# Feed-forward weights turned and their low-rank products added in one PSUM bank, bias rows centred before the loops, early scales in two pieces

## The reference, cut to what matters

```python
x = x + xattn(ctx, ctx, layernorm(x))       # 128 batches x 64 tokens x 128; 16 heads; softmax over the key axis
x = x + ffn(layernorm(x))                   # gamma, beta given for the layer norms inside
# ffn, h = its input:
for blk in range(3):
    i0, i1 = 2 * blk, 2 * blk + 1
    y = qlora(h, i0); y = layernorm(y, gamma[blk], beta[blk]); y = gelu(y)
    y = qlora(y, i1); h = y + h
# qlora(x, i) = x @ W_i.T + bias_i + (x @ la_i.T) @ lb_i.T     W_i = (q_i / 7.5 - 1) * scale_i (groups of 16), rank 32
```

## Time and profile before

| what | value |
|---|---|
| median of three runs | 362.67 us |
| the profiled execution, its own time | 362.27 us |
| its span | 360.4 us |
| PE, DVE busy | 340.1 us (94%), 331.7 us (92%) |
| ACT, POOL busy | 288.2 us (80%), 266.8 us (74%) |
| chain that ended last | PE 62%, DVE 23%, POOL 5%, issue 5%, ACT 3% |

### The profile page before, as it was taken

One profiled execution on the slowest core, in us unless ns is written; L12 is line 12 of the kernel. 1 busy time (PEld: TensorE's weight loads), 2 busy tenths in 40 slices (PEclk: granted clock), 3 DMA queues, 4 the chain that ended last, 5 costly groups with the idle time before them and its releaser, 6 DMA issues.

```text
span 360.4 us, 13093 instructions
## 1 busy us (share of the span) xinstructions
PE 340.1 (94%) x4804; PEld 254.6 (71%) x4804; DVE 331.7 (92%) x821; ACT 288.2 (80%) x585; POOL 266.8 (74%) x288
## 2 busy tenths in 40 slices
PE   7888799999999999999999798988999999999995
PEld 6555367677667667766766566865888888888874
DVE  6899999999999999999999999979999999988774
ACT  4698588788788878878887767668889999999983
POOL 6609488878877977987897999878877788774231
PEclk9999899999999999999999999999999999999999
DMA  7879286467548547745834400000010000210112
GB/s 197 237 238 274 70 255 188 143 202 218 169 137 262 177 136 210 212 154 159 262 132 136 148 4 2 2 1 3 17 45 29 29 29 29 61 32 29 36 54 88
DMA packets 54531, 43.29 MB, mean 120 GB/s; under 512 B 4625, under 2 KB 48609, under 8 KB 54497
## 3 DMA queue, kind: packets, MB, share of 16 engines
q1 hardware_dynamic: 53920, 42.31, 38.8%
q10 hardware_dynamic: 576, 0.53, 0.5%
HBM read 26.05 MB, written 16.78 MB: 119 GB/s over the span
## 4 chain that ended last, share of the span: by engine, by line
PE 62%; DVE 23%; POOL 5%; issue 5%; ACT 3%; DVEq 0%; POOLq 0%; ACTq 0%
PE score_ps L1637 9%; PE att_ps L1600 7%; DVE zsum L847 6%; PE score_ps L1541 5%; DVE negmax L829 5%; PE wo_ps L1379 5%; PE score_ps L1391 3%; PE score_ps L1730 3%; PE work L1723 3%; PE work L1415 3%; POOL probs L524 3%; PE att_ps L1730 3%; PE score_ps L1631 2%; PE work L1428 2%; PE work L1421 2%
## 5 line engine op out<-in xcount | busy, mean ns | idle before, releaser
L524 POOL TENSOR_TENSOR probs<-probs,rz 128x1024 f32<-128x1024 f32 x64 | 136.2, 2141 | 37.0 <-DVE rz L850 36.9
L571 POOL TENSOR_TENSOR rs<-ve,minus_half 128x4 f32<-128x4 f32 (+1 forms) x47 | 55.6, 1184 | 34.3 <-DVE ve L778 24.7
L1139 ACT ACTIVATE probs<-score_ps 128x1024 f32<-128x1024 f32 x64 | 65.6, 1024 | 17.8 <-PE score_ps L1541 17.1
L847 DVE TENSOR_REDUCE zsum<-probs 128x64 f32<-128x1024 f32 x64 | 77.3, 1208 | 1.7 <-ACT probs L1139 1.5
L829 DVE TENSOR_REDUCE negmax<-score_ps 128x64 bf16<-128x1024 f32 x64 | 75.2, 1177 | 0.0
L1379 PEld LDWEIGHTS wo_ps<-wo_t,att_t 128*128 128x128 f32 x256 | 36.9, 191 | 13.4 <-issue 12.0
L1600 PE MATMUL att_ps<-probs,v_diag 128*32 128x64 f32 x2048 | 43.8, 225 | 2.1 <-POOL probs L524 2.1
L1637 PEld LDWEIGHTS score_ps<-lin_t,h 128*128 128x128 f32 x304 | 36.9, 191 | 11.1 <-DVE h L930 7.0
L1221 ACT ACTIVATE z<-score_ps,rs 128x128 f32<-128x128 f32 x152 | 43.5, 382 | 0.6 <-POOL rs L571 0.6
L1541 PE MATMUL score_ps<-negmax,ident_bf 128*128 128x512 bf16 x128 | 39.0, 386 | 4.7 <-DVE negmax L829 4.7
L1600 PEld LDWEIGHTS att_ps<-probs,v_diag 128*32 128x32 f32 x2048 | 33.2, 109 | 12.6 <-POOL probs L524 3.4
(11 more groups left out here) (263 smaller groups left out, 692.6 us busy)
## 6 DMA issues: line engine op xcount, KB each, us to landing
q_parts<-parts SPq DMA_DIRECT2D x15, 512.0 KB, 3.5
k_stack<-k_parts SPq DMA_DIRECT2D x30, 256.0 KB, 3.3
q_stack<-q_parts SPq DMA_DIRECT2D x60, 128.0 KB, 3.0
x_all<-in_x SPq DMA_DIRECT2D x16, 256.0 KB, 3.9
ctx_sb<-in_ctx SPq DMA_DIRECT2D x16, 256.0 KB, 3.7
k_parts<-parts SPq DMA_DIRECT2D x16, 256.0 KB, 2.9
out<-x_all SPq DMA_DIRECT2D x15, 256.0 KB, 2.3
q_parts<-parts SPq DMA_DIRECT2D x4, 128.0 KB, 2.4
```

The costliest lines, as they stand in the source:

```text
L524: nc.gpsimd.tensor_tensor(e[:, :, :, :], e[:, :, :, :], by_query.broadcast_to([P, BANDS, SEQ, ADJ]), ALU.mult).then_inc(s_probs, 1)
L571: nc.gpsimd.tensor_tensor(rs2[v][:, lo:hi], ve2[v][:, lo:hi], minus_half[:, lo:hi], ALU.pow).then_inc(p_rs[v], 1)
L847: nc.vector.tensor_reduce(zsum[q][:, :], probs[(p - 1) % 4][:, :, :, :].rearrange("p u k s -> p k u s"), AX_XY, ALU.add).then_inc(s_zsum, 1)
L1139: nc.scalar.activation(probs[p][:, :, :, :], score_ps[p % 2][:, :].rearrange("p (u s k) -> p u k s", s=ADJ, k=SEQ), ACT.Exp, scale=SCALE). ...
```

## The change

Seven things change.

1. The low-rank products are no longer added by DVE. PE turns the dequantised weight (`w_deq`) into its PSUM bank and adds the low-rank product, with operands swapped, onto it (`turned_layer`). For the even layers `lb` is turned by the product with `centre` instead of a transpose. Layers 1 to 3 are done in the prologue, layer 0 in chunk 0, pair 1, layers 4 and 5 in pair 2. L735 and L740 are gone.
2. The fold of the first layer works on `w_deq` and `la_in`, in the prologue (`folded_first_bias`).
3. The bias rows of the first layers lose their mean in the prologue (`centred_rows`, four DVE instructions ahead of the moments of chunk 1), so the seeds need only one ACT copy, in chunk 1. DVE's five instructions there are gone; its two for `res_cols` move ahead of the first key parts.
4. POOL clears `v_diag[1]` only after the first `negmax`.
5. SP loads `x_all[3]` behind the stores of chunk 1 and the fourth context behind its gathers.
6. In chunk 0 the moments and the scale of input chunk 3 move from pair 1 to pair 2.
7. The early scales are two pieces: `input_variances` (seven POOL instructions) and `input_scales` (two), at places of their own; the moments of chunks 0 and 1 move ahead.

```diff
-X_STATS = {0: (13, 0), 1: (13, 2), 2: (14, 0)}
-X_SCALES = {0: (13, 1), 1: (13, 3), 2: (14, 2)}
+X_STATS = {0: (12, 2), 1: (13, 1), 2: (14, 0)}
+X_VARIANCES = {0: (12, 3), 1: (13, 2), 2: (14, 1)}
+X_SCALES = {0: (13, 0), 1: (13, 3), 2: (14, 2)}
...
+        def moments_slot(c):
+            return 2 if isinstance(c, int) and c == 0 else 1
...
                 gather_first_q(1, s_stack[0])
-                sp.dma_start(x_all[:, 3, :, :], x_t[3]).then_inc(s_xin[3], 16)
                 store_k(1, 1)
                 store_q(1, 1)
-                sp.wait_ge(s_ctx_ps, 2)
-                sp.dma_start(ctx_sb[1][:, :, :], ctx_t[3]).then_inc(s_ctxin[1], 16)
+                sp.dma_start(x_all[:, 3, :, :], x_t[3]).then_inc(s_xin[3], 16)
                 gather_k(1, 1)
                 sp.wait_ge(s_const, 7)
                 gather_q(1, 1)
+                sp.wait_ge(s_ctx_ps, 2)
+                sp.dma_start(ctx_sb[1][:, :, :], ctx_t[3]).then_inc(s_ctxin[1], 16)
...
                 first_scale(2)
+                pool.wait_ge(s_negmax, 1)
                 clear(v_diag[1], s_vzero)
...
-                    if p == 1 and live(c + 3):
+                    if p == moments_slot(c) and live(c + 3):
                         input_variance(c + 3)
+                    input_part(X_VARIANCES, c, p, input_variances)
                     input_part(X_SCALES, c, p, input_scales)
...
+            def centred_rows():
+                nc.vector.tensor_tensor(row_mean[:, 0:1], ident[0:NROWS, ROW_BL + 2:ROW_BL + 3],
+                                        ident[0:NROWS, ROW_BL + 4:ROW_BL + 5], ALU.add)
+                nc.vector.tensor_reduce(row_mean[:, 1:2], rows[:, :], AX_X, ALU.add).then_inc(s_rows_c, 1)
+                dve.wait_ge(s_rows_c, 1)
+                nc.vector.scalar_tensor_tensor(row_mean[:, 2:3], row_mean[:, 1:2], -1.0 / D, row_mean[:, 0:1], ALU.mult,
+                                               ALU.mult).then_inc(s_rows_c, 1)
+                dve.wait_ge(s_rows_c, 2)
+                nc.vector.tensor_scalar(rows_c[:, :], rows[:, :], row_mean[:, 2:3], None, ALU.add).then_inc(s_rows_c, 1)
...
                 dve.wait_ge(s_wready, 4)
+                residual_columns()
                 dve.wait_ge(s_k_ps, 1)
...
                 next_input(0)
                 centred_query_weights()
                 bias_columns()
+                centred_rows()
                 next_input(1)
                 first_key_parts()
                 next_input(2)
                 output_weights()
+                dequantised_weights()
                 low_rank_rows()
                 bias_parts()
-                dequantised_weights()
-                last_effective_weights()
+                folded_first_bias()
...
-                    if isinstance(c, int) and (c, p) == (0, 1):
-                        effective_weights()
...
                     if isinstance(c, int) and (c, p) == (1, 0):
-                        first_layer_seeds()
+                        dve.wait_ge(s_res, 1)
...
+            def turned_layer(i, opens=False):
+                if i % 2 == 0:
+                    nc.tensor.matmul(turned_bank(i), w_deq[:, i, :], centre[:, :], start=opens, stop=False,
+                                     skip_group_check=True)
+                else:
+                    nc.tensor.matmul(turned_bank(i), w_deq[:, i, :], ident[:, :], is_transpose=True, start=opens,
+                                     stop=False, skip_group_check=True)
+                return nc.tensor.matmul(turned_bank(i), la_in[:, i, :], lb_t[:, i, :], start=False, stop=True,
+                                        skip_group_check=True)
+            def first_turned_layers():
+                pe.wait_ge(s_deq, 2)
+                pe.wait_ge(s_lbt, 1)
+                turned_layer(1, opens=True)
+                turned_layer(2)
...
                 project_k(1, 1)
-                low_rank_products(0)
+                first_turned_layers()
                 project_q(1)
                 k_remainder(1, 1)
-                low_rank_products(1)
+                turned_layer(3)
                 q_remainder(1, 1)
```

More of the change, by code:

```diff
@@ L559, in input_scales @@
                 token_variance(0, t + 1, p_xbn, p_xmv, p_xst)
+            def input_scales(t):
                 pool.wait_ge(p_xst, t + 1)
@@ L748, in effective_weights @@
                 dve.wait_ge(s_fold, 2)
+                nc.vector.tensor_scalar(la_mean[:, 1:2], la_mean[:, 0:1], -1.0 / D, None, ALU.mult).then_inc(s_fold, 1)
+                dve.wait_ge(s_fold, 3)
                 nc.vector.tensor_scalar(fold[:, 2:3], fold[:, 1:2], 1.0 / D, None, ALU.mult).then_inc(s_fold, 1)
[L750 to L767 removed]
+                dve.wait_ge(s_fold, 4)
+                nc.vector.tensor_scalar(la_in[:, 0, :], la_in[:, 0, :], la_mean[:, 1:2], None,
+                                        ALU.add).then_inc(s_fold, 1)
+                dve.wait_ge(s_fold, 5)
+                nc.vector.tensor_scalar(w_deq[:, 0, :], w_deq[:, 0, :], fold[:, 2:3], None,
+                                        ALU.add).then_inc(s_fold, 1)
             def combine_layer(v, k):
@@ L991, in transposed, with first_layer_seeds @@
                                      source[:, 0:P].rearrange("p (j h) -> p h j", j=DH), ACT.Copy).then_inc(s_wready, 1)
+            def first_layer_seeds():
+                act.wait_ge(s_seed_ps, 1)
+                nc.scalar.activation(seed[:, :, :].rearrange("p v d -> p (v d)"), wo_ps[:, 2 * P:4 * P],
+                                     ACT.Copy).then_inc(s_seed, 1)
             def transposed_layers(u):
@@ L1111, in prologue @@
                 act.wait_ge(s_wready, 4)
+                nc.scalar.activation(neg_last[:, :], cols[:, ROW_BL + 5:ROW_BL + 6].broadcast_to([P, P]), ACT.Copy,
+                                     scale=-1.0).then_inc(s_neg_last, 1)
                 first_q_part(0, 0, wo_ps, h_q_ps, h_q_hi)
@@ L1128, in prologue @@
                 q_low(1, 1)
-                nc.scalar.activation(neg_last[:, :], cols[:, ROW_BL + 5:ROW_BL + 6].broadcast_to([P, P]), ACT.Copy,
-                                     scale=-1.0).then_inc(s_neg_last, 1)
                 normalised_input(2)
@@ L1150, in chunk @@
                     input_columns(c + 2)
+                if isinstance(c, int) and c == 1:
+                    first_layer_seeds()
                 for u in range(2):
@@ L1336, in low_rank_columns @@
                 ins.then_inc(s_lbt_ps, 2)
-            def low_rank_products(u):
-                if u == 0:
-                    pe.wait_ge(s_lbt, 1)
-                else:
-                    pe.wait_ge(s_wready, 5)
-                for i in range(4 * u, min(4 * u + 4, NLIN)):
-                    ins = nc.tensor.matmul(layer_bank(i), lb_t[:, i, :], la_in[:, i, :], start=True, stop=True)
-                ins.then_inc(s_lora, 1)
-            def transpose_layers(u):
-                if u == 0:
-                    pe.wait_ge(s_weff, 3)
-                    pe.wait_ge(s_const, 5)
-                else:
-                    pe.wait_ge(s_v, 1)
-                for i in range(4 * u, min(4 * u + 4, NLIN), 2):
-                    nc.tensor.matmul(turned_bank(i), w_eff[:, i, :], centre[:, :], start=True, stop=True)
-                    ins = nc.tensor.transpose(turned_bank(i + 1), w_eff[:, i + 1, :], ident[:, :])
-                ins.then_inc(s_lint_ps, 1)
+            def turned_layer(i, opens=False):
+                if i % 2 == 0:
+                    nc.tensor.matmul(turned_bank(i), w_deq[:, i, :], centre[:, :], start=opens, stop=False,
+                                     skip_group_check=True)
+                else:
+                    nc.tensor.matmul(turned_bank(i), w_deq[:, i, :], ident[:, :], is_transpose=True, start=opens,
+                                     stop=False, skip_group_check=True)
+                return nc.tensor.matmul(turned_bank(i), la_in[:, i, :], lb_t[:, i, :], start=False, stop=True,
+                                        skip_group_check=True)
@@ new lines, in first_turned_layers, with first_turned_layer, last_turned_layers @@
+            def first_turned_layers():
[3 more added lines that the diff above has]
+                turned_layer(2)
+            def first_turned_layer():
+                pe.wait_ge(s_fold, 7)
+                turned_layer(0).then_inc(s_lint_ps, 1)
+            def last_turned_layers():
+                pe.wait_ge(s_v, 1)
+                turned_layer(4, opens=True)
+                turned_layer(5).then_inc(s_lint_ps, 1)
```

68 lines of the change are left out of this document (24 added, 44 removed).

## The result

| what | before | after |
|---|---|---|
| median, runs of both taken together | 362.48 us (361.74 to 363.77, 8 runs) | 359.04 us (358.77 to 360.88, 8 runs) |
| the profiled execution, its own time | 362.27 us | 359.06 us |
| its span | 360.4 us | 357.2 us |

A forecast was written before the change was run, and what follows sets the result against it. The prediction took DVE to bound the start, with PE and DVE both full in the middle. Its terms +1.50, -4.66 and -0.5 summed to -3.66 us, giving 358.8 us, with a range of 356.5 to 361.2.

The forecast's parts named there:

- What this delay meets: Prologue: held L681 delays chunk 1's moments, the first key part by 1.56 us and the first maximum by 1.50.
- the argument by 78 ns: Prologue: 78 ns taken off L639's 287 for its PSUM scalar leave 209, so L681 runs double-rate and is held.
- -4.66: First maximum to chunk 2's: removed DVE work counts in full, 1.61 us in chunk 0 and 3.05 in chunk 1.
- rival 3: Chunks 0 and 1: a new wait for x_all[3], the gathers or POOL's scale returns 1 to 2.5 us; chance 0.10.
- The end of DVE's prologue: Before the first maximum: 0.74 of wait and addition and a 1.56 stall go, fold and three instructions come, -0.69 us.
- PE's turned layers: PE's prologue: they wait for lb_t until about 17.4 and end by 18.4, under the landing at 20.93.
- The order of SP at nothing: Chunks 0 and 1: gathers land with 1 us to spare, x_all[3] about when the moments want it; no cost.
- The low clock behind the seeds: Chunk 1: cost PE up to 1.7 us of work, mostly made good behind DVE; counted as nothing.
- -0.5 for chunks 12 to 14: Seven POOL instructions stand one product earlier, PE's 1.33 us wait goes; -0.5 us, bounds -1.3 and +0.4.
- Rival 1: Prologue: L681 is not held or slips in between two memsets; first maximum at 19.87, 357.1 to 357.5 us; chance 0.22.
- Rival 2 (the clock): Prologue: PE's 1.92 us wait lowers its clock, adding 1 to 1.7 us, 359.8 to 360.5 us; chance 0.22.
- Rival 4: Prologue: clock falls at 11.85 and stays low until the first scores; slower than before, 365.3 us; chance 0.04.

The follow-up runs named there:

- wait_behind: The changed kernel with one more wait of DVE, for the held L681, ahead of the moments of chunk 1: 360.92 us, ratio 0.9962 to the kernel before.
- rows_late: The changed kernel with L681 moved behind POOL's memsets, to the head of bias_parts: 358.56 us, ratio 0.9905 to the kernel before.
- seeds_only: The kernel before with only the centred bias rows, the moved res_cols instructions and the seeds as one ACT copy: 359.94 us, ratio 0.9939.
- pool_unheld: The changed kernel with POOL clearing v_diag[1] without waiting for the first maximum: 359.04 us, ratio 0.9891 to the kernel before.
- layers_late: The changed kernel with layers 1 to 3 turned in chunk 0, pair 1, and not in the prologue: 360.76 us, ratio 0.9955 to the kernel before.
- sp_order_old: The changed kernel with SP's loads in the order of before: 358.89 us, ratio 0.9905 to the kernel before.
- moments_slot_old: The changed kernel with moments and scale of input chunk 3 back in pair 1 of chunk 0, SP's new order kept: 362.51 us, ratio 0.9990.
- old_scales: The changed kernel with moments, variances and scales of the early inputs where they were before: 359.63 us, ratio 0.9936 to the kernel before.
- layers_again: The changed kernel with layers 1 to 3 turned in the prologue and once more in chunk 0, pair 1: 360.71 us, ratio 0.9956.
- two_layers_short: The changed kernel without layer 4's turning and the low-rank products of layers 4 and 5 (result not the reference's): 359.17 us, ratio 0.9936.

## Why the prediction was right, and where it was not

The time was forecast at 358.8 us and is 359.04; the sum was -3.66 against -3.20 in the profiled executions. Three of its terms are off, by -0.59, +1.27 and -0.24 us, and cancel in part: that the time came within 0.3 us of its forecast is partly luck.

- **"What this delay meets", +1.50, measured +0.91.** The step that failed is "starting at 9.20 they end at 10.74": the moments ended at 9.27 already, and the key part was 0.64 late, not 1.56. L681 itself did what the row of L679 said (8 of the 11 profiled executions that have it there end it at 9.2 to 9.3). That it is held shows its kind; it does not show the argument by 78 ns, whose two rows differ in output type and partitions as well as in the scalar. With a wait behind it (`wait_behind`) the forecast position is met. The first maximum is 0.27 later than the key part explains; in `rows_late`, whose key part is 0.15 us earlier than before, the first scores still start at 19.95 and not at 19.37. ACT issues the gather of `k_stack` at 14.62 there and at 14.55 before, but from issue to landing it takes 3.5 to 4.5 us where it took 3.7, so most of what is lost lies between issue and landing. What makes that longer stays open.
- **"-4.66", measured -3.39.** Its two parts do not fare alike. The seeds gave 3.07 for 3.05 (`seeds_only`). The addition and the fold gave 0.35 for 1.61: mis-sized by 1.26. The failed sentence is "PE's work for a pair of chunks 0 and 1 is under DVE's, the exponentials come a few tenths of a us before their sums". That was read from a trace in which moments, addition and fold stood between the second maximum and the first sum, 22.14 to 24.53, and covered the wait for the first exponential. With all of them gone from there, one moved and the others removed, that wait came out, 0.74 us, and with it 0.34 ahead of 33.28 and 0.22 ahead of 37.07. In size this is rival 3, "a new wait in chunks 0 and 1" (1 to 2.5 us), but not in its cause: it named the load of `x_all[3]`, the gathers and POOL's scale, and DVE waited for exponentials. It was also taken as an alternative to the forecast and was a part of it.
- **The end of DVE's prologue, -0.69**, measured -1.23 (19.28 - 19.87 - 0.64), mostly since the fold and its three instructions take 1.14 us and not 1.61, was rightly not on the path: DVE is free at 19.28 and waits 1.51 us for the first scores. `pool_unheld` shows that its largest item, the stall, was worth nothing in the end.
- **PE's turned layers** were put at 1 us and take 2.1 (16.55 to 18.03 and from 19.21 on); the three products of 32 rows take some 0.4 us each. It costs nothing, since the landing comes no sooner (`layers_late`), but by luck rather than by the sentence.
- **The order of SP at nothing**: right (`sp_order_old`), and incomplete. It is paid for by the pair of the moments; without that DVE waits 3.42 us and the stretch is 4.22 longer (`moments_slot_old`). The prediction said that the load lands "about when DVE's moments, one pair later, want it", and did not price what happens without.
- **The low clock behind the seeds, counted at nothing.** In the profiled execution that holds: DVE has no gap there, and `seeds_only` gave the row's 3.05 and no more. It does not follow for every execution. Of the 81 executions of the kernel before in the four groups, the 39 with a mean granted clock of 0.998 or more have medians of 361.67 to 361.87 by group, the 42 others 362.59 to 363.09: the lower clock goes with about 1 us.
- **-0.5 for chunks 12 to 14**: measured -0.74, and 0.71 by `old_scales`. The wait for POOL goes; a wait of 0.54 for DVE stands in its place, as forecast under "late next".
- **Rival 1** is the case in 3 of 11 profiled executions, by its second form (L681 slips in between two memsets), as told below; the first maximum is then at 20.17 to 20.43, not at its 19.87. **Rival 2 (the clock)** did not come in the profiled execution: PE waited 1.00 us at 10.91 for the key part, and the granted clock is 1.00 from 0 to 46. Nor did it with the wait that the rival had in mind: in `wait_behind` PE waits 1.86 us at 11.71, and the clock of that execution is 1.00 from 0 to 46 as well (where seven other executions of that kernel lost some clock is open). **Rival 4** needed rival 2.
- **The chance of "faster"**: the forecast, rivals 1 and 2 and half of rival 3 add up to 0.91, where the text has 0.86 in round numbers.

Of the signs named, L681, the cast, the clock, the missing waits at 38 and in chunk 14 came; L731 came at 10.03 for 10.95, the first maximum at 20.78 for 21.4 and that of chunk 2 at 44.37 for 43.7, and DVE has the gaps that the text said would disprove it.

## What to carry to other kernels

Work that is removed from a full engine is worth its duration only where nothing else was waiting under it: look for the first consumer behind it, and ask when its input would have been ready. A fill-in instruction (here the moments) belongs into the wait that is uncovered, together with the load that feeds it. To learn which of two full engines holds a stretch, add work and take work away; here either direction alone would have given a wrong answer, since two paths were level. And look at the mean granted clock of the single executions before explaining a median: in `wait_behind` half of the loss went with it.

## What the runs showed of the hardware

**A held DVE instruction does not keep the ones behind it from being worked off.** L681 begins at 7.48 and is held until 9.27. The four moments behind it start 0.20 us later, at 7.68 to 8.27, and all end with it; the next instruction, which needs them, starts at 9.34, where it would be another 0.87 us later if they had only begun at 9.27. So their work is done under the hold, and their ends come with its end. The Trainium skill (Perfetto Trace Analysis: Optimizing Scalar/DVE Operations) says that the write-acknowledgement half of a DVE instruction overlaps with the next one; the overlapping records here agree with that and are drawn out to 1.59 us, but which half of L681 is drawn out no run shows. In `wait_behind` a semaphore wait on the held instruction made DVE stop.

**The hold does not always last for all the memsets.** In 8 of the 11 profiled executions with L681 in that place it ended behind all four memsets; in `old_scales`, `layers_again` and `two_layers_short` it got in after the second, at 8.28 to 8.36. Timeline of DVE in `old_scales`:

```profile
7.62 0.70 DVE L681 TENSOR_SCALAR rows_c<-rows,row_mean 16x128 f32<-16x128 f32 x1
7.82 0.85 DVE L623 BATCH_NORM_STATS2 stats<-x_all 128x6 f32<-128x128 f32 x4
```

The four memsets took 1.98 us there (7.27 on) where they take 1.91, and the first maximum came 0.35 us sooner, at 20.43. What decides it was not found. The Trainium skill (SBUF — State Buffer: SBUF: two separate sides) has the lock held "for the whole instruction" by whichever starts first. The three executions agree in so far as L681 gets in between two memsets; the other eight do not, unless back-to-back memsets leave no room between them. Nor do the starts of the records decide it: in `wait_behind`, `pool_unheld`, `seeds_only`, `layers_again` and `layers_late` L681 begins at 7.02 to 7.13 and the first memset at 7.22 or 7.23, and L681 is held all the same.
